# First step of the aggregation in fp32 on unconverted adj, adj in pieces until step 31, LayerNorm of tiles 0 to 3 on VectorE

## The reference

```python
h = jnp.maximum(_layernorm(x, axis=-1), 0.0)      # x: 8192 x 128
support = jnp.matmul(h, W)                        # W: 128 x 128
out = jnp.matmul(adj, support) + b                # adj: 8192 x 8192, fp32
x = x + jax.nn.relu(out)
```

## Time and profile before

| | us |
|---|---|
| median of 3 runs | 731.24 (731.15 to 732.17) |
| profiled execution, own time | 730.47 |
| its span | 728.7 |
| PE busy / DVE busy / ACT busy / POOL busy | 713.4 / 616.6 / 526.2 / 131.2 |
| first product starts at | 5.97 |
| last product ends near | 722 |
| DMA over the span | 281.59 MB, 386 GB/s |

### The profile page before, as it was taken

The page is one execution under the profiler, slowest core; times in us unless marked ns, Lnnn a source line. Parts: engine busy times, 40 slices in busy tenths (PEclk is TensorE's granted clock), DMA queues, the critical chain, the costliest instruction groups (busy, mean ns, idle before and its releaser), DMA issues.

```text
span 728.7 us, 7676 instructions
## 1 busy us (share of the span) xinstructions
PE 713.4 (98%) x3120; PEld 587.3 (81%) x3120; DVE 616.6 (85%) x277; ACT 526.2 (72%) x355; POOL 131.2 (18%) x86
## 2 busy tenths in 40 slices
PE   4999999999999999999999999999999999999997
PEld 2788888888888888888888888888888888888885
DVE  4999998999899888888879888888888888888894
ACT  6888888778888767766667776667666666777772
POOL 3454575554445400000000000000000000000000
PEclk9999999999999999999999999999999999999999
DMA  8999999999999999999999999999999999999982
GB/s 320 425 423 422 424 421 401 400 406 398 398 403 385 382 396 397 414 379 397 366 416 410 394 408 390 382 385 396 378 391 376 392 385 385 398 410 400 390 346 72
DMA packets 32724, 281.59 MB, mean 386 GB/s; under 512 B 3760, under 2 KB 4144, under 8 KB 11056
## 3 DMA queue, kind: packets, MB, share of 16 engines
q1 hardware_dynamic: 32688, 281.10, 96.6%
HBM read 276.89 MB, written 4.19 MB: 386 GB/s over the span
## 4 chain that ended last, share of the span: by engine, by line
PE 96%; DMA 1%; SPq 1%; DVE 1%; ACT 1%; issue 0%
PE banks L454 95%; DMA raw<-adj 1%; PE banks L472 1%; PE banks L474 1%; PE banks L473 1%; DVE low L425 0%; ACT high L314 0%; SPq L163 0%; SPq L182 0%; SPq L191 0%; SPq L190 0%; DVE sum_low L384 0%; ACT relu_out L284 0%; DVE x_sb L391 0%; ACT sum_high L276 0%
## 5 line engine op out<-in xcount | busy, mean ns | idle before, releaser
L425 DVE TENSOR_TENSOR low<-raw,high 128x3072 fp32r<-128x3072 f32 (+1 forms) x170 | 568.8, 3347 | 95.1 <-PE banks L454 83.0
L314 ACT ACTIVATE high<-raw 128x3072 fp32r<-128x3072 f32 (+1 forms) x170 | 470.4, 2767 | 171.9 <-DMA raw<-adj 157.0
L454 PE MATMUL banks<-high,h_high 128*128 128x512 f32 x1024 | 263.6, 391 | 10.2 <-DVE h_low L367 6.0
L454 PE MATMUL banks<-high,h_low 128*128 128x512 f32 x1024 | 262.4, 390 | 0.0
L454 PE MATMUL banks<-low,h_high 128*128 128x512 f32 x1024 | 261.1, 390 | 0.4 <-DVE low L425 0.4
L454 PEld LDWEIGHTS banks<-high,h_high 128*128 128x128 f32 x1024 | 192.9, 188 | 53.0 <-ACT h_high L261 5.9
L454 PEld LDWEIGHTS banks<-low,h_high 128*128 128x128 f32 x1024 | 192.9, 188 | 40.9 <-DVE low L425 0.8
L454 PEld LDWEIGHTS banks<-high,h_low 128*128 128x128 f32 x1024 | 193.1, 189 | 39.9
L240 POOL TENSOR_SCALAR z_sb<-x_sb,neg_mean,rstd 128x128 f32<-128x128 f32 x64 | 109.2, 1718 | 1.8
L232 POOL TENSOR_TENSOR rstd<-var_eps,minus_half 128x4 f32<-128x4 f32 (+2 forms) x17 | 21.7, 1274 | 110.8 <-DVE var_eps L360 110.8
L253 ACT ACTIVATE squares<-x_sb,neg_mean 128x128 f32<-128x128 f32 x64 | 24.9, 390 | 10.4 <-DVE neg_mean L354 10.4
(11 more groups left out here) (17 smaller groups left out, 26.7 us busy)
## 6 DMA issues: line engine op xcount, KB each, us to landing
raw<-adj SPq DMA_DIRECT2D x169, 1536.0 KB, 8.7
x_sb<-x_blocks SPq DMA_DIRECT2D x16, 256.0 KB, 8.2
out_blocks<-x_sb SPq DMA_DIRECT2D x16, 256.0 KB, 8.8
x_sb<-x_rows SPq DMA_DIRECT2D x15, 256.0 KB, 9.1
raw<-adj SPq DMA_DIRECT2D x2, 512.0 KB, 7.0
raw<-adj SPq DMA_DIRECT2D x2, 256.0 KB, 3.9
raw<-adj_end SPq DMA_DIRECT2D x1, 512.0 KB, 7.6
raw<-adj_end SPq DMA_DIRECT2D x2, 256.0 KB, 4.9
```

The source lines that it names most:

```text
L314: nc.scalar.activation(high[:, t % HIGH_SLOTS, 0:columns(t)], raw[:, t % RAW_SLOTS, 0:columns(t)], ACT.Copy).then_inc(high_ready, 1)
L425: nc.vector.tensor_tensor(low[:, t % LOW_SLOTS, 0:columns(t)], raw[:, t % RAW_SLOTS, 0:columns(t)], high[:, t % HIGH_SLOTS, 0:columns(t)]. ...
L454: return nc.tensor.matmul(banks[:, FIRST_BANK[g] + c, :], h[:, (t - FIRST_STEP[g]) * DEPTHS[g] + k, :], tile[:, slot, at:at + BANK], start ...
```

## The change

- **Step 0** is not converted. PE multiplies raw fp32 by h_first (tile 0 of h, plain fp32): six products of 512 columns, each of which the engine makes in four passes. SP waits for these products before it reuses raw slot 0 (t = 4).
- **Tile 0 of h** comes from DVE alone but for the power on POOL: bn_stats, bn_aggr, two small operations, centre and rectify, scale. Tiles 1 to 3 still take mean and squares as before, but DVE centres, rectifies and writes h_high and h_low. Batch 2 (tiles 4 to 7) takes its statistics from DVE too. The halves of tile 0 for the later groups are formed by DVE after step 9.
- **adj** comes in separate, contiguous arrays and transfers: 1, 1, 2, 2 blocks at step 0, three pieces of two blocks in steps 1 to 5 (rows of 4 KB), two of three blocks in steps 6 to 31 (rows of 6 KB), whole steps from 32 on (the last one in halves as before). ACT and DVE convert piece by piece. PE runs the products with high piece by piece, then those with low piece by piece.
- **x** lies in one contiguous array for each batch. ACT issues batches 0, 1 and 2 ahead of its own work; SP issues adj's step 0 and 1 first, then batch 3 before step 2, batch 4 before step 3, batch 5 before step 5 as before. W and b are loaded after step 7, and their conversions moved to steps 9 and 13.
- **Zero products**: before step 0, PE runs eight fp32 products of 128 columns on a zeroed tile, into a bank that group 1 opens later.

```diff
-OPENING = [1, 1, 2, 2]
...
+EARLY = 4
+WARMING = 8
...
+def split_of(t):
+
+    if t == 0:
+        return [1, 1, 2, 2]
+    if t < 6:
+        return [2, 2, 2]
+    if t < 32:
+        return [3, 3]
+    g = group_of(t)
+    return [1] * WIDTHS[g] if t == LAST else [WIDTHS[g]]
...
+                if t in (2, 3):
+                    load_x(t + 1)
+                if t >= 4 and t % 4 == 1 and t // 4 + 4 < len(BATCHES):
+                    load_x(t // 4 + 4)
+                if t == RAW_SLOTS:
+
+                    sp.wait_ge(products_done, 1)
+                if t > RAW_SLOTS:
+
+                    sp.wait_ge(low_ready, halved(t - RAW_SLOTS))
+                for i in range(len(split_of(t))):
+                    load_piece(t, i)
+                if t == 7:
+                    sp.dma_start(W_sb[:, :], W).then_inc(params_landed, 16)
+                    sp.dma_start(bias[:, :], b).then_inc(params_landed, 16)
                 n = drained_at(t, 0)
                 if n is not None:
...
+                if t > HIGH_SLOTS:
+
+                    act.wait_ge(low_ready, halved(t - HIGH_SLOTS))
+                    act.wait_ge(high_used, t - HIGH_SLOTS)
+                for i in range(len(split_of(t))):
+                    cols = columns_of(t, i)
+                    act.wait_ge(raw_landed[t % RAW_SLOTS][i], landed(t, i))
+                    nc.scalar.activation(high[:, t % HIGH_SLOTS, cols], raw[:, t % RAW_SLOTS, cols],
                                          ACT.Copy).then_inc(high_ready, 1)
...
+            def statistics(at, t, j):
+                cols = slice(t % 4 * P, t % 4 * P + P)
+                nc.vector.bn_stats(stats[:, at, :], x_sb[:, x_slot(j), cols]).then_inc(stats_ready, 1)
+
+            def aggregate(at):
+                nc.vector.bn_aggr(moments[:, at, :], stats[:, at, :]).then_inc(moments_ready, 1)
+
+            def var_and_mean(at, first, end):
+                here = slice(at, at + end - first)
+                nc.vector.tensor_scalar(var_eps[:, first:end], moments[:, here, 1], EPS, None,
+                                        ALU.add).then_inc(var_ready, 1)
+                nc.vector.tensor_scalar(neg_mean[:, first:end], moments[:, here, 0], -1.0, None,
+                                        ALU.mult).then_inc(centre_ready, 1)
+
+            def centre(t):
+                cols = slice(t % 4 * P, t % 4 * P + P)
+                nc.vector.tensor_scalar(z_sb[:, 0, cols], x_sb[:, 0, cols], neg_mean[:, t:t + 1], 0.0,
+                                        ALU.add, ALU.max).then_inc(centred, 1)
...
             def rectified_low(j):
                 first, end = BATCHES[j]
-                at = first % 4
-                dve.wait_ge(h_high_ready, j + 1)
+                dve.wait_ge(h_high_ready, j - 1)
                 nc.vector.scalar_tensor_tensor(h_low[:, first:end, :],
-                                               z_sb[:, x_slot(j) % Z_SLOTS, at * P:(at + end - first) * P]
+                                               z_sb[:, x_slot(j) % Z_SLOTS, :]
                                                .rearrange("p (t d) -> p t d", d=P),
...
+            statistics(0, 0, 0)
+            dve.wait_ge(stats_ready, 1)
+            aggregate(0)
+            dve.wait_ge(moments_ready, 1)
+            var_and_mean(0, 0, 1)
+            dve.wait_ge(centre_ready, 1)
+            centre(0)
+            dve.wait_ge(centred, 1)
+            dve.wait_ge(rstd_ready, 1)
+            nc.vector.tensor_scalar(h_first[:, :], z_sb[:, 0, 0:P], rstd[:, 0:1], None,
+                                    ALU.mult).then_inc(h_first_ready, 1)
             mean(1)
...
+            dve.wait_ge(mean_ready, 1)
+            for t in range(1, 4):
+                centre(t)
+            dve.wait_ge(x_landed[1], 16)
+            for t in range(4, 8):
+                statistics(t - 3, t, 2)
             variance(1)
...
+            dve.wait_ge(stats_ready, 5)
+            for t in range(4, 8):
+                aggregate(t - 3)
+            dve.wait_ge(moments_ready, 5)
+            var_and_mean(1, 4, 8)
+            dve.wait_ge(centred, EARLY)
+            dve.wait_ge(rstd_ready, 2)
+            for t in range(1, 4):
+                early_halves(t)
...
+                for i in range(len(split_of(t))):
+                    cols = columns_of(t, i)
+                    dve.wait_ge(high_ready, halved(t, i))
+                    nc.vector.tensor_tensor(low[:, t % LOW_SLOTS, cols], raw[:, t % RAW_SLOTS, cols],
+                                            high[:, t % HIGH_SLOTS, cols].bitcast(F32),
                                             ALU.subtract).then_inc(low_ready, 1)
...
+            for _ in range(WARMING):
+                nc.tensor.matmul(banks[:, PSUM_BANKS - 1, 0:P], warm[:, :], warm[:, :], start=True, stop=True)
+
+
+            pe.wait_ge(h_first_ready, 1)
+            for i in range(len(split_of(0))):
+                pe.wait_ge(raw_landed[0][i], 16)
+                for c in blocks_of(0, i):
+                    last = nc.tensor.matmul(banks[:, FIRST_BANK[0] + c, :], h_first[:, :],
+                                            raw[:, 0, c * BANK:(c + 1) * BANK], start=True, stop=False)
             last.then_inc(products_done, 1)
 
...
+                for i in pieces:
+                    pe.wait_ge(high_ready, halved(t, i))
+                    if i == 0:
+                        high_is_there(t)
+                    for k in depths:
+                        for c in blocks_of(t, i):
+                            product(t, c, k, h_high, high, t % HIGH_SLOTS, start=opens and k == 0)
+                    if i == 0:
+                        low_is_there(t)
+                    for k in depths:
+                        for c in blocks_of(t, i):
+                            last = product(t, c, k, h_low, high, t % HIGH_SLOTS)
...
+                for i in pieces:
+                    pe.wait_ge(low_ready, halved(t, i))
+                    for k in depths:
+                        for c in blocks_of(t, i):
+                            last = product(t, c, k, h_high, low, t % LOW_SLOTS,
+                                           stop=closes and k == depth_of(t) - 1)
...
```

More of the change, by code:

```diff
@@ L55, in depth_of, with blocks_of, columns_of, halved @@
     return min(DEPTHS[g], TILES - (t - FIRST_STEP[g]) * DEPTHS[g])
+def split_of(t):
[7 more added lines that the diff above has]
+    return [1] * WIDTHS[g] if t == LAST else [WIDTHS[g]]
+def blocks_of(t, i):
+    start = sum(split_of(t)[:i])
+    return range(start, start + split_of(t)[i])
+def columns_of(t, i):
+    blocks = blocks_of(t, i)
+    deep = depth_of(t) * BANK
+    return slice(blocks[0] * deep, (blocks[-1] + 1) * deep)
+HALVED_BEFORE = [0, 0]
+def halved(t, i=None):
+    while len(HALVED_BEFORE) <= t:
+        HALVED_BEFORE.append(HALVED_BEFORE[-1] + len(split_of(len(HALVED_BEFORE) - 1)))
+    return HALVED_BEFORE[t] + (len(split_of(t)) if i is None else i + 1)
+def landed(t, i):
+    return 16 * len([s for s in range(t % RAW_SLOTS, t + 1, RAW_SLOTS) if i < len(split_of(s))])
+def squares_at(t):
+    if t in (2, 3):
+        return 3, range(8 + (t - 2) * 2, 10 + (t - 2) * 2)
+    j = t // 4 + 3
+    if t >= 4 and t % 4 in (1, 2) and j < len(BATCHES):
+        at = BATCHES[j][0] + (t % 4 - 1) * 2
+        return j, range(at, at + 2)
+    return None
+def mean_at(t):
+    j = 3 if t == 1 else t // 4 + 3 if t >= 4 and t % 4 == 0 else None
+    return j if j is not None and j < len(BATCHES) else None
+def variance_at(t):
+    j = 3 if t == 3 else t // 4 + 3 if t >= 4 and t % 4 == 2 else None
+    return j if j is not None and j < len(BATCHES) else None
+def rectified_at(t):
+    j = t // 4 + 2 if t % 4 == 2 else None
+    return j if j is not None and j < len(BATCHES) else None
 def x_slot(j):
@@ L145, in columns @@
             return WIDTHS[g] * depth_of(t) * BANK
-        def landed(t):
-            return 16 * len([s for s in range(1, t + 1) if s % RAW_SLOTS == t % RAW_SLOTS])
         def x_landed_count(j):
@@ L258, in rectify @@
                 first, end = BATCHES[j]
-                act.wait_ge(z_ready, end)
-                at = first % 4
+                act.wait_ge(z_ready, end - EARLY)
                 nc.scalar.activation(h_high[:, first:end, :],
-                                     z_sb[:, x_slot(j) % Z_SLOTS, at * P:(at + end - first) * P]
-                                     .rearrange("p (t d) -> p t d", d=P),
+                                     z_sb[:, x_slot(j) % Z_SLOTS, :].rearrange("p (t d) -> p t d", d=P),
                                      ACT.Relu).then_inc(h_high_ready, 1)
-            def opening(i):
-                start = sum(OPENING[:i])
-                cols = slice(start * BANK, (start + OPENING[i]) * BANK)
-                act.wait_ge(opening_landed[i], 16)
-                nc.scalar.activation(high[:, 0, cols], raw[:, 0, cols], ACT.Copy).then_inc(opening_high, 1)
             def sum_to_high(n):
@@ L371, in rectified_low @@
```

(20 more changed lines are left out.)

282 lines of the change are left out of this document (106 added, 176 removed).

## The result

The changed kernel takes 725.7 us (median; 725.36 to 726.77) against 731.19 (730.61 to 732.17) for the kernel before beside it: a ratio of 0.9921, 95% interval 0.9901 to 0.994. The forecast was 726.5. The profiled execution of after takes 725.54 us with a span of 723.7, against 730.47 and 728.7; the forecast for it was 725.8.

A forecast was written before the change was run, and what follows sets the result against it. PE, busy 98%, bounds the kernel, so only an earlier gapless start counts: step 9 ends at 51.6 instead of 56.3, gain 4.7 us. 730.47 - 4.7 = 725.8 profiled, 726.5 against the median; range 724.0 to 730.4.

The forecast's parts named there:

- (1): Opening, step 0's arrival: 0.4 us sooner from bounds of nothing and 1.4; piece 3 lands at 10.0 (8.6 to 10.8).
- rival E: Opening: piece 3 lands at 8.6, arrivals come 1.4 us sooner, gain 6.1 us, time 725.1; chance 0.11.
- (2): Opening, tile 0 of h: new chain takes 1.8 us with hand-overs, so PE may start near 4.5 instead of 5.97.
- (3): Step 0's products: each fp32 product takes 0.91 us at fast spacing, 1.71 at slow; step 0 ends at 12.0.
- Rival C: Opening: zero products fail, spacing stays slow, step 0 ends at 15.1; only 0.8 us gained, 730.4; chance 0.06.
- (4): Step 1: 4 KB rows give 410 GB/s, 6 KB rows 416; it ends at 17.2 against 23.62, 6.4 us sooner.
- Rivals A: Steps in pieces, felt at step 32: below 395 GB/s the change is slower, 734.3 at 384 GB/s; chance 0.09.
- B: Stream or opening: 395 to 410 GB/s, or piece 3 at 11.5; gains near 2.5 us, 728.7; chance 0.16.
- (5): Steps 2 to 9: waits of 0.43, 0.43, 0.2, 0.6 us at steps 2, 3, 5, 6; step 9 ends at 51.6, gain 4.7.
- (6): Step 32, whole again: lands at 137.3; low wanted at 144.1, ready at 143.5, so it holds with 0.6 us to spare.
- (7): DVE's work per step becomes 3.5 us; every four steps 15.7 us in 16.3, covered narrowly; early statistics end near 12.4.
- Rival D: DVE: 0.1 us more hand-over per half, 16.5 us in 16.3; about 2 us lost by step 31, 728.4; chance 0.05.

The follow-up runs named there:

- the run with x first: Changed kernel with SP issuing batch 0 of x ahead of adj's first piece, ACT only batches 1 and 2: 726.25 us, ratio 0.9937.
- late x: Changed kernel with the loads of x from batch 5 on before steps 7, 11, 15 instead of 5, 9, 13: 726.55 us, ratio 0.9936.
- late x with three pieces: Changed kernel with x loads from batch 5 on two steps later, two pieces up to step 47, three until step 9: 725.59 us, ratio 0.9914.
- late x with pieces until 47: Changed kernel with x loads from batch 5 on two steps later and two pieces up to step 47 instead of 31: 725.4 us, ratio 0.9914.

## Why the prediction was right, point by point

The time came out right, but in part by luck. This is when the last piece of each step landed in the kernel after (issue plus time to landing), beside the forecast, in us:

| step | 0 | 1 | 2 | 3 | 4 | 5 | 6 |
|---|---|---|---|---|---|---|---|
| forecast | 10.0 | 13.85 | 18.4 | 22.9 | 26.7 | 31.3 | 35.0 |
| landed | 8.1 | 11.9 | 16.5 | 21.0 | 24.8 | 30.7 | 34.4 |

- **(1) Arrivals.** The weakest term. Step 0's last piece landed at 8.1, where I had 10.0 (8.6 to 10.8). The mis-sized part is the second queue, which I took at 0.4 us and which is worth about 1.0 to 1.4 of arrivals (312 GB/s against 382 to 409); kernels with the same first transfers landed it at 8.1 to 9.6, so this execution was also an early one. Up to step 4 the arrivals then keep their lead of 1.9 us, since the rate is as forecast. At step 5 they lose 1.3 of it: the last piece lands 2.7 us behind its second instead of 1.3. The transfers did not slow down (18.7 us at 411 GB/s are 7.7 MB, and steps 2 to 5 with three loads of x are 7.1), so something else moved beside this piece, which my line, with the transfers strictly one behind the other, does not have. The two misses nearly cancel. Without the late piece PE would have had no wait at steps 5 and 6 (step 6's last piece ready at 34.65, wanted at 34.69), and step 10 would have started at about 17.01 + 8 x 4.08 = 49.65 (an estimate), 1.6 us earlier. So rival E's condition came true (step 0's last piece at 8.6 or earlier) and its gain of 6.1 did not.
- **(2) PE's start** was 5.79, not 4.5. The chain on VectorE and POOL takes 1.96 us (forecast 1.8), but x lands at 3.8 instead of 2.7, on its own queue beside piece 0. I had not seen that x would land later; that the engines are shared is the likely reason, and no run isolates it. The later start costs nothing, as the run with x first shows.
- **(3) The fp32 product** costs 0.86 us at the short spacing (forecast 0.91), 1.71 at the long one (1.71). The spacing became short at 9.4, two us later than assumed; step 0 ends at 12.46 (12.0). Rival C, that the zero products don't work, half came true and had no price: the run without them ends where the kernel after does.
- **(4) Rates.** 4 KB rows were to give 410 GB/s, 6 KB rows 416; measured 411 and 416 to 418, and 415 from 35 to 130 us, just what I had asked for. The price per row read from the loads of x carried the forecast: it made the landing of step 32, 100 us later, 137.3; measured 136.99. Rivals A (below 395) and B (395 to 410 or a late opening) fall with it. The Trainium skill, DMA: Bandwidth & Descriptors, section "Measured", gives 341 GB/s for a transfer of 1 MB and asks for at least 1 MiB. Its table is for transfers that GpSimd issues. The traces don't agree for those that SP queues behind one another: 0.52 and 0.79 MB at a time move 411 and 416, and the measurement decides.
- **(5) Steps 2 to 9.** I forecast waits of 0.43, 0.43, 0.2 and 0.6 us at steps 2, 3, 5 and 6; there are none at 2 and 3 and about 0.9 and 0.6 at 5 and 6. Together 1.66 against 1.6, and this agreement is the luck of (1): at steps 2 and 3 the data was 1.9 us early, so that PE did not wait, and at step 5 it met a delay that I had not foreseen. Step 10 was to start at 51.6 and starts at 51.28; the gain was 5.1 instead of 4.7.
- **(6) Staying there.** Held, with 0.05 us lost at step 33 where I had 0.6 to spare for low. The late x shows how near the edge this is: a landing 1.4 us later costs 1.3 us (0.3 ahead at step 10, 1.0 behind at step 35). The wait at step 32 that I gave as a sign did not come.
- **(7) VectorE** held: 1.769 us for half a step, 3.54 a step (forecast 3.5), and PE waits for it nowhere by more than 0.05. The low part of step 1's first piece starts at 10.80, before the 12.4 that I had. Rival D had no share; its 2 us don't follow from its own numbers either, since 0.2 us every four steps is 1.5 by step 31.

Undoing one part at a time costs, at step 10 and by the median: 3.7 and 3.2 us (pieces), 3.4 and 2.1 to 2.9 (fp32 step 0), 1.2 to 1.5 and 1.3 (x on ACT), 0.4 and 0.2 (contiguous arrays), 0.3 and 0.1 (zero products); pieces only until 11 cost 2.7 between steps 10 and 35, and 2.6 by the median. The costs of the arrays and the zero products are within what landings scatter. The sum is above the 5.1 that they bring together: each is worth what it is only while the others hold.

Left open are two scatters of the landings. The first transfers are the same in the kernel after and in five others, but step 0's last piece lands at 8.1 and 8.4 (after, no zero products) or at 9.4 to 9.6 (pieces until 11, and the three kernels with late x). And one piece between 28 and 35 us lands 1.3 to 1.5 us late: the last of step 5 in after and in late x with three pieces, the second of step 5 with pieces until 11, the last of step 6 without zero products; in late x with pieces until 31 or 47 none does. No experiment isolates either. Each can move PE's line by up to 1.4 us in a single execution, so a difference under that between two profiles, without one in the medians, shows nothing.

## What to carry to other kernels

When the engine that limits a kernel is 98% busy, look for its last wait in the opening, and shorten what lies between the landing and that engine: here the conversion of a whole step, cut to a third. Keep the cut until the transfers are one whole step's conversion ahead, and compute when that is from the two rates. Speed ahead of the next arrival (a faster clock, an earlier first product) is lost there. Before an agreement between a forecast and a time is called understanding, compare the terms as well: here two misses of 1.9 and 1.3 us nearly cancelled.

## What the runs showed of the hardware

- **Two issuing queues** moved more in the opening than one: 382 to 409 GB/s in six kernels against 312 and 329 in two executions with the same transfers on one queue, from 3 to 9 us, and 372 against 284 in the kernel before. The Trainium skill, DMA: Bandwidth & Descriptors, section "Rules for kernel authors", says that spreading transfers over issuing engines doesn't help bandwidth; these runs show otherwise for the first 9 us. From 10 to 36 us the rate is 411 either way, so it is an effect of the opening. Which property of the small rows makes it was not tried, nor the order of issue apart from the queue.
- **The first load of x** (64 KB, issued at 0.7 either way) landed at 3.8 on the second queue, beside the pieces of adj on the first, and at 2.5 to 2.7 when it was first on the only queue. The share of each cause was not tried.
- **The same opening, two clocks**: with the zero products in place, the short spacing came with the first fp32 product in four kernels (slices of whole arrays, pieces until 11, late x, late x with three pieces) and about 3.6 us later, near 9.4 to 9.5, in the kernel after and in late x with pieces until 47, with the granted clock at 1.00 in all of them. What decides it was not tried; PE's program up to the end of step 0 is the same in these six.
- **Time to landing scatters**: the same four first transfers of adj, with the same x beside them, were all landed at 8.1 us in one kernel and at 9.6 in another.
- **The power on POOL**, 128x4, took 4.18 us once, in the run with step 0 converted, where VectorE was behind; the mean of the kernel after is 1.33. That the two hang together was not tested.
